# A graph network's message stage: where the hundredth of each row is made, and in which order ScalarE works

## The reference, cut to what matters

```python
src_full = jnp.concatenate([src, dst])
dst_full = jnp.concatenate([dst, src])
ef_full = jnp.concatenate([ef, ef], axis=0)
edge_in = jnp.concatenate([nf[src_full], nf[dst_full], ef_full], axis=-1)
msg = leaky_relu(edge_in @ We1) @ We2          # leaky_relu: x where x >= 0, else 0.01 * x
red = jax.ops.segment_sum(msg, dst_full, num_segments=nf.shape[0])
out_nf = leaky_relu(jnp.concatenate([nf, red], axis=-1) @ Wn1) @ Wn2
```

## Time and profile before

| | |
|---|---|
| median of 3 runs | 6084.42 us |
| profiled execution, its own time | 6084.27 us |
| its span in the trace | 6082.4 us |
| POOL busy | 4167.2 us (69%) |
| PE busy | 3522.1 us (58%) |
| DVE busy | 3392.1 us (56%) |
| ACT busy | 1253.6 us (21%) |
| mean granted PE clock | 0.727 of full speed |

### The profile page before, as it was taken

How to read it: one execution, slowest core, us unless ns; L and a number is a source line. 1 busy time by engine, 2 the same in 40 slices (tenths; PEclk the granted TensorE clock), 3 DMA queues, 4 the chain that set the end, 5 groups by cost and what they waited for, 6 DMA issues and landing times. The chain is left out here.

```text
span 6082.4 us, 100738 instructions
## 1 busy us (share of the span) xinstructions
PE 3522.1 (58%) x16911; PEld 2533.7 (42%) x16912; DVE 3392.1 (56%) x10967; ACT 1253.6 (21%) x3300; POOL 4167.2 (69%) x3995
## 2 busy tenths in 40 slices
PE   0242222221677775246776777777777777776767
PEld 0121111110566665243544454444444444444446
DVE  4642222222666667894655566565556656565554
ACT  0220000000455554333111111111111111111112
POOL 3147777775677776422888888888888888888870
PEclk9875555555555555668888888888888888888879
DMA  2255555552455555126877887877788878878874
GB/s 53 85 148 146 145 144 143 145 146 62 115 128 128 128 128 165 44 54 180 171 166 166 168 171 166 170 167 166 165 171 169 166 167 170 168 166 168 171 137 134
DMA packets 917011, 874.25 MB, mean 144 GB/s; under 512 B 231003, under 2 KB 767995, under 8 KB 916759
## 3 DMA queue, kind: packets, MB, share of 16 engines
q0 software_dynamic: 238848, 434.00, 36.0%
q1 hardware_dynamic: 641111, 406.09, 25.2%
q10 hardware_dynamic: 37008, 33.70, 2.5%
HBM read 623.00 MB, written 250.35 MB: 144 GB/s over the span
## 5 line engine op out<-in xcount | busy, mean ns | idle before, releaser
L1439 POOL DMA_INDIRECT sums<-msg_bsum,msg_sidx x928 | 1561.2, 1682 | 308.1 <-issue 249.4
L1581 PEld LDWEIGHTS msg_fwd_ps<-msg_onehot,msg_hid 128*128 128x128 f32 x3712 | 639.7, 224 | 1413.6 <-issue 1299.0
L1448 POOL DMA_INDIRECT msg_ga<-ab,msg_idx x928 | 953.9, 1028 | 390.2 <-issue 234.7
L1594 PE MATMUL msg_pre_ps<-msg_rw,msg_lt 128*128 128x512 f32 x1856 | 1109.0, 683 | 45.1 <-DVE msg_xs L1518 36.2
L1581 PE MATMUL msg_fwd_ps<-msg_onehot,msg_hid 128*128 128x64 f32 x3712 | 624.4, 298 | 810.2 <-DVE l_fwd L1500 801.0
L688 POOL DMA_INDIRECT max_xe<-rows,max_idx x832 | 800.0, 962 | 422.8 <-issue 253.3
L1552 ACT ACTIVATE msg_bsum<-msg_bwd_ps 128x256 f32<-128x256 f32 x928 | 356.1, 384 | 2567.9 <-PE msg_bwd_ps L1583 2551.0
L864 POOL TENSOR_SCALAR att_keyhot<-k_ramp,att_keys 128x128 f32<-128x128 f32 x1028 | 616.0, 616 | 279.8 <-ACT att_keys L936 279.8
L1583 PE MATMUL msg_bwd_ps<-msg_hid,msg_same 128*128 128x256 f32 x1856 | 709.3, 469 | 0.0
L976 PE MATMUL att_sum_ps<-att_px,att_keyhot 128*128 128x136 f32 x2056 | 559.1, 453 | 230.2 <-DVE att_px L898 225.0
L1525 DVE SCALAR_TENSOR_TENSOR msg_hid<-msg_xs 128x512 f32<-128x512 f32 x928 | 639.1, 689 | 0.1
(11 more groups left out here) (265 smaller groups left out, 5013.3 us busy)
## 6 DMA issues: line engine op xcount, KB each, us to landing
msg_rw<-ab SPq DMA_DIRECT2D x928, 128.0 KB
att_xe<-xe SPq DMA_DIRECT2D x1028, 72.0 KB, 2.5
xe<-max_xe SPq DMA_DIRECT2D x104, 576.0 KB, 3.5
att_keyrow<-key ACTq DMA_DIRECT2D x257, 128.0 KB, 3.5
msg_lt<-in_efT SPq DMA_DIRECT2D x928, 32.0 KB
msg_ga<-ab,msg_idx POOLq DMA_INDIRECT x928
sums<-msg_bsum,msg_sidx POOLq DMA_INDIRECT x928
rows<-node_rows SPq DMA_DIRECT2D x50, 288.0 KB, 2.4
```

The costliest lines, as they stand in the source:

```text
L1439: pool.indirect_dma_start(T.sums[u % 2], bass.IndirectOffsetOnAxis(ap=sidx[:, b, u:u + 1], axis=0), bsum[:, b, u, :], None, compute_op=ALU ...
L1448: pool.indirect_dma_start(ga[:, b, u, :], None, T.ab, bass.IndirectOffsetOnAxis(ap=idx[:, b, u:u + 1], axis=0)).then_inc(s_ga[b], 16)
L1581: pe.matmul(fwd_ps[u % 2][:, q * WIN:(q + 1) * WIN], hid[:, b % 2, u, HID + q * P:HID + (q + 1) * P], onehot[:, b, u, :], start=True, stop ...
L1594: pe.matmul(pre_ps[u % 2][:, :], lt[:, b, u, :], rw[:, b % 2, u, :], start=True, stop=True).then_inc(s_pre, 1)
```

## The change

Three edits in the message stage, and one of names:

1. `hid` is no longer made from xs twice. ACT reads xs, multiplies it by 0.01 and writes the result to a new PSUM tile `low_ps` (two buffers, one bank each). DVE then takes the larger of xs (SBUF) and `low_ps` (PSUM) with a `tensor_tensor`, behind a new wait on ACT (`s_low`).
2. `fwd_ps` and `bwd_ps` of a step share one PSUM bank (`both_ps`), which frees the two banks for `low_ps`. ACT's copy of the backward part now waits until DVE's add of that step is done (`s_acc`), not only for PE.
3. ACT's stages are reordered. Before: indices, sums (lag 4), move (lag 2). Now: indices, steps (lag 5). A `steps` call does for each of the four steps the copy of the step three behind, then `low`; after the second it moves the next group's one-hots. As seen from the moves and the copies, the index copies stand further ahead by one or two groups. `move(0, 0)` stands in front of everything.
4. In the mix phase one semaphore (`s_wc`) is folded into another (`s_adiag`); what waits for what is unchanged.

```diff
-        fwd_ps = [ph.ps(f"fwd_ps{b}", [P, 2 * WIN]) for b in range(2)]
-        bwd_ps = [ph.ps(f"bwd_ps{b}", [P, HID]) for b in range(2)]
+        both_ps = [ph.ps(f"both_ps{b}", [P, 2 * WIN + HID]) for b in range(2)]
+        fwd_ps = [t[:, 0:2 * WIN] for t in both_ps]
+        bwd_ps = [t[:, 2 * WIN:2 * WIN + HID] for t in both_ps]
+        low_ps = [ph.ps(f"low_ps{b}", [P, 2 * HID]) for b in range(2)]
...
-                    dve.wait_ge(s_x, n + 1)
+                    dve.wait_ge(s_low, n + 1)
                     if past(j, 2):
                         dve.wait_ge(s_edge, (j - 2) * U + u + 1)
-                    dve.scalar_tensor_tensor(hid[:, b % 2, u, :], xs[:, u % 2, :], SLOPE1, xs[:, u % 2, :],
-                                             ALU.mult, ALU.max).then_inc(s_hid, 1)
+                    dve.tensor_tensor(hid[:, b % 2, u, :], xs[:, u % 2, :], low_ps[u % 2][:, :], ALU.max).then_inc(s_hid, 1)
...
-            def sums(j, b):
+            def low(n, j, u):
+                act.wait_ge(s_x, n + 1)
+                if past(j, 1) or u >= 2:
+                    act.wait_ge(s_hid, n - 1)
+                act.activation(low_ps[u % 2][:, :], xs[:, u % 2, :], ACT.Copy, scale=SLOPE1).then_inc(s_low, 1)
+
+            def sums(n, j, b, u):
+                act.wait_ge(s_acc, n + 2)
+                if past(j, RG):
+                    act.wait_ge(s_sum[u], (j - RG + 1) * 16)
+                act.activation(bsum[:, b, u, :], bwd_ps[u % 2][:, :], ACT.Copy).then_inc(s_bs, 1)
+
+            def steps(j, b):
                 for u in range(U):
-                    act.wait_ge(s_edge, j * U + u + 1)
-                    if past(j, RG):
-                        act.wait_ge(s_sum[u], (j - RG + 1) * 16)
-                    act.activation(bsum[:, b, u, :], bwd_ps[u % 2][:, :], ACT.Copy).then_inc(s_bs, 1)
-
-            pipeline(act, GROUPS, RG, [(0, indices), (4, sums), (2, move)])
+                    n = j * U + u
+                    if u >= ADD_LAG:
+                        sums(n - ADD_LAG, j, b, u - ADD_LAG)
+                    elif past(j, 1):
+                        sums(n - ADD_LAG, j - 1, (b - 1) % RG, u - ADD_LAG + U)
+                    low(n, j, u)
+                    if u == 1 and not (isinstance(j, int) and j == GROUPS - 1):
+                        move(j + 1, (b + 1) % RG)
+
+            move(0, 0)
+            pipeline(act, GROUPS, RG, [(0, indices), (5, steps)])
+            for n in range(STEPS - ADD_LAG, STEPS):
+                sums(n, GROUPS - 1, (GROUPS - 1) % RG, n % U)
```

More of the change, by code:

```diff
@@ L1073, in node_update @@
         f_ps = ph.ps("f_ps", [P, H])
-        s_w, s_adiag, s_fold, s_wc, s_gT, s_gTs, s_h, s_ent, s_c, s_arg, s_ex, s_out, s_gend = (
-            ph.sem(n) for n in ("w", "adiag", "fold", "wc", "gT", "gTs", "h", "ent", "c", "arg", "ex", "out", "gend"))
+        s_w, s_adiag, s_fold, s_gT, s_gTs, s_h, s_ent, s_c, s_arg, s_ex, s_out, s_gend = (
+            ph.sem(n) for n in ("w", "adiag", "fold", "gT", "gTs", "h", "ent", "c", "arg", "ex", "out", "gend"))
         s_g, s_xb, s_stat = ph.sem("g"), ph.sem("xb"), ph.sem("stat")
@@ L1125, in _ @@
             dve.wait_ge(s_fold, 1)
-            dve.tensor_copy(w_c[:, C:CR], f_ps[:, :]).then_inc(s_wc, 1)
+            dve.tensor_copy(w_c[:, C:CR], f_ps[:, :]).then_inc(s_adiag, 1)
             dve.wait_ge(s_adiag, 2)
@@ L1238, in _ @@
             pe.matmul(f_ps[:, :], w_cT[:, :], adiag[:, :], start=True, stop=True).then_inc(s_fold, 1)
-            pe.wait_ge(s_wc, 1)
+            pe.wait_ge(s_adiag, 3)
             def transpose(t, b):
@@ L1396, in edge_messages @@
         s_sum = [ph.sem(f"sum{u}") for u in range(U)]
-        (s_w, s_idx, s_oh, s_tr, s_oT, s_same, s_row, s_pre, s_x, s_hid, s_edge, s_acc, s_bs, s_rc) = (
-            ph.sem(n) for n in ("w", "idx", "oh", "tr", "oT", "same", "row", "pre", "x", "hid", "edge", "acc", "bs", "rc"))
+        (s_w, s_idx, s_oh, s_tr, s_oT, s_same, s_row, s_pre, s_x, s_low, s_hid, s_edge, s_acc, s_bs, s_rc) = (
+            ph.sem(n) for n in ("w", "idx", "oh", "tr", "oT", "same", "row", "pre", "x", "low", "hid", "edge", "acc", "bs", "rc"))
         block = ph.block()
```

## The result

The changed kernel takes 5971.54 us, the median of four runs (5964.70 to 5974.02); the kernel before takes 6084.82 us (6084.12 to 6086.06). The ratio is 0.9813, with a 95% interval of 0.9801 to 0.9825: 113 us faster, where 106 had been forecast. On a second chip the same pair gave 0.9814 (0.9801 to 0.9828).

What follows compares the result with a forecast made beforehand. POOL's own issuing of gathers and scatters was taken to bound the message stage. Against the profiled 6084.3 us, -117 (hid's operand) + 4 (start) + 3 (DMA) + 4 (one-hots) = -106 gave 5978 us, range 5960 to 6050.

Steps and rivals of the forecast that it cites:

- The bound: Message stage: POOL's own issuing of one gather and one scatter a step sets the period, 3.32 us a step.
- Edit 1: hid from SBUF and PSUM: POOL is no longer held at its start by two SBUF operands, -117 us (bounds 0 and 122).
- hid's own time: DVE's hid with one PSUM operand: expected to take 0.69 us again.
- The new wait: hid waits for ACT's low: DVE's step grows from 1.74 to 2.29 us, a group to 11.5 us, under POOL's 12.8.
- ACT's order: Reordered ACT in the message stage: DVE works a group (12.8 us) later than before, and POOL does not feel it.
- The start: Start of the message stage: index copy behind the first move, first scatter at 2861.7 instead of 2858.32; +4 us (0 to 20).
- The two small terms: Message stage: DMA busier, +3 us (0 to 15); DVE's one-hots may hold POOL more, +4 us (-4 to +30).
- C: Rival: POOL's hold has another cause and stays at 3.32 us a step, only the start costs; 6088 us, chance 0.06.
- A: Rival: slow handoffs make the DVE and ACT chain bind, slower than before, from a 2.73 us step; 6139 us, chance 0.10.
- B: Rival: the DVE and ACT chain binds between the two periods, at a 2.65 us step; 6013 us, chance 0.13.

Runs made afterwards that it cites:

- E1: The changed kernel with low written to a one-buffer SBUF tile instead of PSUM, so hid reads two SBUF tensors again; ratio 0.9988 to the kernel before.
- E3: The kernel before with both products sharing a PSUM bank and hid made from xs and a PSUM tile of zeros, without low; ratio 0.9848.
- E6: The changed kernel with ACT making low twice in a row, so hid comes later in every step; 6170.92 us, ratio 1.0149 to the kernel before.
- E4: The changed kernel with lag 4 instead of 5 for ACT's steps; ratio 0.9857 to the kernel before.

## Why the prediction was right

- **The bound.** POOL's own issuing was the period, and is. Its gaps did not change: 290.3 us plus 402.0 less the wait of 119.4 at the stage's start make 0.62 us a step, before 0.62.
- **Edit 1.** Forecast -117 us from the starts in a hid; the means give -120, the few us at the one-hots and elsewhere included. The cause that had been inferred from coincidence is shown by E1 and E3.
- **hid's own time.** 687 ns with a PSUM operand, 689 without, as the row for xs had said; in E1 the same instruction from two SBUF tiles takes 693. The 62 cycles more that the Trainium skill (VectorE: DVE Perf Modes, the errata section) charges for a PSUM source do not show here.
- **The new wait.** Forecast a step of 2.29 us, measured 2.22: `low` takes 600 ns and not 630, and both handoffs are 0.03 to 0.04 us. The rest of a group was taken as 2.35 us, and E6 gives 2.3. So by this estimate a group of DVE is 4 x 2.22 + 2.3 = 11.2 us, under POOL's 12.8: the slack is about 0.4 us a step, not 0.3, and the chain would bind from (12.8 - 2.3) / 4 = 2.63 us a step on. E6, at 2.85 us, is beyond that point; no run stands close to it.
- **ACT's order.** Forecast: DVE works a group later and POOL does not feel it. DVE's waits for scatters fell from 747.7 us to 13.1, and ACT now waits for gathers instead:

```profile
ACT msg_idx L1540 <- DMA msg_ga<-ab,msg_idx: 905.2, 218, 9.3
...
DVE msg_sidx L1495 <- DMA sums<-msg_bsum,msg_sidx: 13.1, 44, 0.3
```

  The same slack, under another name. E4 shows that the lag is not needed for it.
- **The start.** From the first xs to the first scatter it is 8.1 us, before 4.5: +3.6, forecast +4.

```profile
2849.02 0.35 DVE L1519 TENSOR_TENSOR msg_xs<-msg_pre_ps,msg_ga 128x256 f32<-128x256 f32 x1
...
2857.12 1.63 POOL L1441 DMA_INDIRECT sums<-msg_bsum,msg_sidx  x1 [2.08 <-DVE msg_xs L1520]
```

  The first xs itself came 4.8 us earlier than in the profiled execution before, where the prediction had said that it does not move. Of the edits only the merged semaphore lies ahead of it, and no run has that edit alone, so whether it has a part in this is not shown. It is one reason why the two profiled executions differ by 119.6 us and the medians by 113.
- **The two small terms** were too dear. The stage is 117.9 us shorter from first to last scatter where the means give 120, so all that was not the length of POOL's instructions cost 2 us there, where +3 had been put for DMA alone. The +4 for the one-hots did not come: they hold POOL for 3.7 us over 3000 to 5780 us, before 4.2 over 3000 to 5890. Added up from these measured terms, -120 + 2 + 3.6 = -114 us, where the medians give -113 and the forecast was -106.

Of the rivals, C is excluded by E1 and E3, A and B by the step's size: they needed 2.73 and 2.65 us, and it is 2.22.

## What to carry to other kernels

If one engine issues back to back, compare the mean and the median of its instructions: the difference can be a hold that no wait shows, and setting the long instances against what the other engines run at their start names a suspect. Coincidence is not yet the cause: here it took the operand moved by itself, and moved back. Work may be moved onto an idle engine at a loss for the engine that seems relieved, if this changes where an operand is read. Before lengthening a chain beside the bound, compute how much it may grow; one run with the new piece doubled tests that figure, and here it found the rest of a group mis-sized.

## What the runs showed of the hardware that I had not expected

- The hold is shorter than what is left of the DVE instruction by 0.12 to 0.13 us: 0.57 us left and 0.44 over the median, 0.38 and 0.25, 0.63 and 0.51, and in E1 0.25 and 0.13. It is so all through the stage before (3000 to 5890 us): of 382 transfers that start in a hid with more than 0.13 us left, 373 are held for what is left less 0.10 to 0.14 us; of 36 with less left, none is held.
- The other nine start within 0.04 us of the hid's start. They are not held, and the hid is longer instead, up to 0.76 us:

```profile
4799.69 0.76 DVE L1525 SCALAR_TENSOR_TENSOR msg_hid<-msg_xs 128x512 f32<-128x512 f32 x1
4799.72 1.59 POOL L1439 DMA_INDIRECT sums<-msg_bsum,msg_sidx  x1 [0.30 <-issue]
```

  A hid that starts up to 0.02 us behind a transfer's start is longer as well, 0.70 to 0.72 us; from 0.03 us behind it on, a hid takes its usual 0.69 us. None of these holds the transfer. So both sides can be the one that is held, but POOL holds DVE only for a moment at its own start and not for its 1 to 1.6 us. The Trainium skill (SBUF — State Buffer, "Who interferes with whom") says that whoever issues first has the shared ports for the whole instruction; it says so of VectorE's two-port modes, and the prediction took it for any instruction with two SBUF inputs. With DVE as the first these rows come close to that, up to the 0.13 us; with POOL as the first they do not.
- ScalarE's copy of 512 columns is 600 ns from SBUF to PSUM, against 630 ns from SBUF to SBUF; in E1, where only the destination of `low` differs, it is 628 ns:

```profile
L1552 ACT ACTIVATE msg_low_sb<-msg_xs 128x512 f32<-128x512 f32 x883 | 554.7, 628 | 220.5 <-DVE msg_xs L1520 156.6 <-issue 63.8
```
